# VectorE mends a row ahead of its share of the second list's sort, in the second half of each step

## What is computed

```python
a_src = (h * att_src).sum(-1)
a_dst = (h * att_dst).sum(-1)
e = leaky_relu(a_src[src] + a_dst[dst], negative_slope=0.2)
e_max = segment_max(e, dst)
ee = exp(e - e_max[dst])
denom = segment_sum(ee, dst)
alpha = ee / (denom[dst] + 1e-16)
agg = segment_sum(h[src] * alpha[:, :, None], dst) + b_gat
...
scores = layernorm(agg).mean(1)          # per expert
w = softmax(top_k(scores, 2))
out = sum over experts of g[e] * (gelu(x @ W1[e] + b1[e]) @ W2[e] + b2[e])
```

## Time and profile before

| what | us |
|---|---|
| median of 3 runs | 2843.73 |
| lowest and highest run | 2842.95, 2855.72 |
| profiled execution, its own time | 2834.66 |
| span of the profiled execution, first to last instruction | 2832.8 |
| busy: VectorE | 2124.0 |
| busy: GpSimd | 1202.6 |
| busy: TensorE matmul | 1002.3 |
| busy: ScalarE | 780.2 |

### The profile page before, as it was taken

The page is one execution under the profiler, slowest core; times in us unless marked ns, Lnnn a source line. Parts: engine busy times, 40 slices in busy tenths (PEclk is TensorE's granted clock), DMA queues, the critical chain, the costliest instruction groups (busy, mean ns, idle before and its releaser), DMA issues.

```text
span 2832.8 us, 22266 instructions
## 1 busy us (share of the span) xinstructions
PE 1002.3 (35%) x4867; PEld 675.7 (24%) x4867; DVE 2124.0 (75%) x4081; ACT 780.2 (28%) x1624; POOL 1202.6 (42%) x1234
## 2 busy tenths in 40 slices
PE   6778777499922110099543322350000000000000
PEld 3455445266611110066322221230000000000000
DVE  5989999999789992999488888875633412822888
ACT  3555555244411110044332222221000000000344
POOL 0000000000000005777777764777777777736750
PEclk8766777699955555599775666675555555555555
DMA  2222324992200002133231212124212113342676
GB/s 62 67 67 71 82 70 178 393 138 74 74 15 0 0 0 27 25 83 82 61 47 35 43 37 40 39 46 41 36 20 24 20 10 24 46 42 82 188 240 226
DMA packets 259502, 202.29 MB, mean 71 GB/s; under 512 B 101592, under 2 KB 207445, under 8 KB 258902
## 3 DMA queue, kind: packets, MB, share of 16 engines
q1 hardware_dynamic: 189766, 114.21, 17.2%
q0 software_dynamic: 46336, 44.61, 8.8%
q10 hardware_dynamic: 23314, 42.60, 4.7%
HBM read 94.51 MB, written 107.07 MB: 71 GB/s over the span
## 4 chain that ended last, share of the span: by engine, by line
DVE 28%; PE 21%; POOL 18%; DVEq 14%; issue 10%; ACT 5%; DMA 3%; ACTq 1%; SPq 0%; POOLq 0%
POOL sb_rows_g L782 16%; PE bank L1022 7%; DVE sb_xi L1678 7%; PE bank L1012 6%; DVEq L1694 5%; DVE sb_xi L1685 3%; DVE sb_inv L1383 2%; PE bank L938 2%; DVE sb_hid_y L1518 2%; DVEq L1414 2%; PE bank L1001 2%; DVEq L1404 2%; DVE sb_y_new L2172 1%; PE bank L1019 1%; DVE sb_new L1907 1%
## 5 line engine op out<-in xcount | busy, mean ns | idle before, releaser
L782 POOL DMA_INDIRECT sb_rows_g<-scr_node,sb_srcs x1024 | 1001.4, 978 | 312.1 <-issue 311.7
L1685 DVE TENSOR_TENSOR sb_xi<-sb_xi 128x512 f32<-128x512 f32 (+2 forms) x852 | 427.2, 568 | 46.7 <-ACT sb_xi L1171 33.0
L1001 PE MATMUL bank<-sb_ident,sb_xi 128*128 128x128 f32 x448 | 99.5, 410 | 532.6 <-DVE sb_xi L1685 280.3
L1678 DVE TENSOR_TENSOR sb_xi<-sb_xi 128x1024 f32<-128x1024 f32 (+2 forms) x258 | 243.5, 944 | 27.5 <-ACT sb_xi L1176 8.7
L1022 PE MATMUL bank<-sb_w,sb_hid_y 128*128 128x128 f32 x2048 | 262.6, 281 | 0.0
L782 POOL DMA_INDIRECT sb_hid_y<-scr_level,sb_row_at x8 | 7.9, 985 | 597.3 <-DVE sb_row_at L1442 595.1
L1012 PE MATMUL bank<-sb_tnT_in,sb_w 128*128 128x512 f32 x512 | 238.5, 618 | 57.7 <-DVE sb_sinks L1790 33.5
L1679 DVE TENSOR_TENSOR sb_xi<-sb_xi 128x1024 f32<-128x1024 f32 (+2 forms) x258 | 245.7, 952 | 0.0
L1022 PEld LDWEIGHTS bank<-sb_w,sb_hid_y 128*128 128x128 f32 x2048 | 238.2, 191 | 29.0 <-issue 29.0
L1194 ACT ACTIVATE sb_hid_y<-bank,sb_b1c 128x512 f32<-128x512 f32 x256 | 163.6, 691 | 233.4 <-PE bank L1012 231.5
L1001 PEld LDWEIGHTS bank<-sb_ident,sb_xi 128*128 128x128 f32 x448 | 85.6, 216 | 545.0 <-DVE sb_xi L1685 286.8
(11 more groups left out here) (340 smaller groups left out, 2127.0 us busy)
## 6 DMA issues: line engine op xcount, KB each, us to landing
scr_expert_out<-sb_y_new ACTq DMA_DIRECT2D x64, 512.0 KB, 3.8
sb_y_in<-scr_expert_out SPq DMA_DIRECT2D x32, 1024.0 KB, 6.7
scr_state<-sb_zeros POOLq DMA_DIRECT2D x6, 4096.0 KB, 55.5
sb_rows_g<-scr_node,sb_srcs POOLq DMA_INDIRECT x1024
scr_state<-sb_state SPq DMA_DIRECT2D x16, 768.0 KB, 6.4
scr_tnT<-sb_tnT SPq DMA_DIRECT2D x34, 256.0 KB, 2.0
sb_tnT_in<-scr_tnT ACTq DMA_DIRECT2D x34, 256.0 KB, 2.7
sb_xa<-in_x SPq DMA_DIRECT2D x64, 128.0 KB, 2.5
```

The lines of the kernel that those rows point to most:

```text
L782: pool.indirect_dma_start(to, None, table, bass.IndirectOffsetOnAxis(ap=index, axis=0), **kw).then_inc(s, 16)
L1001: last = pe.transpose(bank[b][:, m * P:(m + 1) * P], src[:, (4 * b + m) * P:(4 * b + m + 1) * P], ident[:, :])
L1678: dve.tensor_tensor(vb[:, :, 0], va[:, :, 0], va[:, :, 1], ALU.min)
L1685: last = dve.tensor_tensor(vb[:, :, d, :, c], va[:, :, d, :, 0], va[:, :, d, :, 1], ALU.min if c == d else ALU.max)
```

## The change

The two lines that mend in a second half now stand first in `half`, on both engines that take part: VectorE's `mend(k - 2)` ahead of the sort's levels and of the search's parts, and ScalarE's `fix_exponentials(k - 2)` ahead of the exchanges' copies and the experts' chunks. What an instruction does is unchanged, as is the number of instructions. The queues of GpSimd, SyncE and TensorE are in the same order as before. In the loop (steps 4 and 5) nothing stands between the old place and the new one, so those steps are unchanged. Four halves have another order: (2, 1) and (3, 1), where the mend passes two levels of the sort; (6, 1), where it passes `find_rank`; and (7, 1), where it passes `find_nodes` and `own_terms`.

```diff
             def half(k, u, j, pair, b):
+                if some(k) and u == 1 and (not isinstance(k, int) or k > 1):
+                    fix_exponentials(k - 2)
                 end = EXCHANGES + SORTED_BY.get((j, u), 0)
                 if end > done[0]:
                     exchanges(done[0], end)
...
-                if some(k):
-                    if u == 0:
-                        chain_exponentials(k - 1)
-                    elif not isinstance(k, int) or k > 1:
-                        fix_exponentials(k - 2)
+                if some(k) and u == 0:
+                    chain_exponentials(k - 1)
                 place_around(k, u, pair, 2 * b + u)
                 edge_exponentials(k, u)
...
             def half(k, u, j, pair, b):
+                if some(k) and u == 1 and (not isinstance(k, int) or k > 1):
+                    mend(k - 2, b)
                 end = SORTED_BY.get((j, u), 0)
                 if end > done[0]:
                     sort_levels(1, done[0], end)
...
-                if some(k):
-                    if u == 0:
-                        chain_runs(k - 1, 1 - b)
-                    elif not isinstance(k, int) or k > 1:
-                        mend(k - 2, b)
+                if some(k) and u == 0:
+                    chain_runs(k - 1, 1 - b)
                 edge_scans(k, u, j, pair, b)
```

## The result

The changed kernel takes **2804.59 us** (median of 4 runs, 2799.65 to 2811.89), the kernel before, on the same chip, 2843.34 us (median of 4 runs). The ratio is 0.9862, with a 95% interval of 0.9825 to 0.9899. The prediction said 2804.7 us, within 2794 to 2818. The profiled execution took 2799.65 us with a span of 2797.8 us, where that of before took 2834.66 us with 2832.8 us.

What follows compares the result with a forecast made beforehand. GpSimd's in-order gather queue was taken to bound the kernel, with one 40.6 us hole at a mended row's store. Filling it gains 37.6 to 40.6 us, taken as 39: median 2843.73 becomes 2804.7 us, range 2794 to 2818.

Steps and rivals of the forecast that it cites:

- What bounds: GpSimd's gather queue sets the pace; its one hole, 40.6 us at the first mended row's store, delays everything behind.
- The mend in (2, 1): On VectorE, begins at 1680.1 and fits the 1.95 us gap before the sort, delaying the sort 0.3 us.
- The store, the mend in (3, 1), and what is next: GpSimd's first store no longer waits; second mend ends 21.8 us ahead of its store; no new wait follows.
- The gathers that fill the hole: Beside the sort of (2, 1), 30 slightly slower gathers fill the hole; gain 37.6 to 40.6 us, taken as 39.
- The rule against the change: Skill's SBUF contention rule: if it held for gathers and sort, the hole takes hardly any gather, gain near 0.
- VectorE's cover: In half (5, 1) VectorE keeps 35 us of waiting as cover; each microsecond beyond is paid, slower than before from 74.
- the mend holds the sort: Rival, 2%: VectorE's early mend waits and delays the sort and later work; slower, for example 2860 us at 90 us lost.
- The sum of VectorE's waits for rows: Sign over the whole kernel: the sum stays more or less the same, (5, 0)'s wait gone, (5, 1)'s near 35 us.
- Halves (6, 1) and (7, 1): Mend passes parts of the search: 2 us earlier or less later, under row waits of 60.5 and 19.34 us.

Runs made afterwards that it cites:

- the second execution: The changed kernel run once more without any edit, in rounds with the kernel before: ratio 0.9877, stage (first search gather to last gather of rows) 1385.2 us.
- a hole of 11 us: Changed kernel with the mends of (2, 1) and (3, 1) between the sort's two levels: first store waits 11.13 us, ratio 0.9918 to the kernel before.
- the experiment with one move alone: Changed kernel with only the mend of (2, 1) moved, the others left late: ratio 0.9988 to the kernel before, second store waits 37.75 us.
- the ten gathers: Ten extra GpSimd gathers in half (1, 0), result unused: added to the kernel before, ratio 1.0010; added to the changed kernel, 0.9948 to the kernel before.
- 151 us: Changed kernel with 116 extra VectorE operations in half (5, 1), result unused, taking 150.9 us: ratio 1.0030 to the kernel before.
- 20 operations more: Changed kernel with 20 extra VectorE operations in half (5, 1), result unused: ratio 0.9871 to the kernel before.
- 60 more: Changed kernel with 60 extra VectorE operations in half (5, 1), result unused, 78.1 us in all: ratio 0.9888 to the kernel before.
- last mend earlier: Changed kernel with the mend of step 6 and its row's fetch also moved ahead of the trips behind the last rows: ratio 0.9846 to the kernel before.

## Why the prediction was right, and where it was not

*What bounds.* Right. Without the hole of 40.6 us the stage was 36.9 us shorter, and 30.0 us in the second execution. With one of the two moves the hole goes to the next store or stays, and a hole of 11 us costs 6 to 13.

*The mend in (2, 1).* Right: 1.9 us in VectorE's gap, with a delay of the sort of 0.2 us where 0.3 was taken. Its place, 1680.1, was off by 3.3 us, of which 2.5 are the later start of the stage.

*The store, the mend in (3, 1), and what is next.* Right: no store waits, the second mend ends 23 us ahead where 21.8 were forecast, and the experiment with one move alone shows 37.75 us of wait where the prediction worked out 1896.6 - 1859.1 = 37.5.

*The gathers that fill the hole.* Here the forecast had the terms wrong, though it did not show in the first time. It was 39 us, out of 37.6 to 40.6: of the 40.6 us the gathers beside the sort were to eat 1.6, at most 3.0. By the medians the first measurement gained 38.75 us; with the changed kernel again it was 31.6, and the stages of the two gained 36.9 and 30.0. Split at the first store, the stage shows where the rest went (us):

| | before | changed | changed, again |
|---|---|---|---|
| up to the first store, without its wait | 602.2 | 602.6 | 608.7 |
| from the first store on | 772.4 | 775.2 | 776.1 |

From the first store on, the changed kernel paid 2.9 and 3.7 us. But the 576 gathers of rows there took 0.2 us less and 0.5 us more than before: they cost nothing to speak of. What grew are transfers that had no term at all. The first gathers of a half (`sb_adw`) took 1.4 and 3.4 us more, and in the first execution the first two stores took 1.50 and 1.68 us instead of 1.02.

The second missing term is larger. Up to the first store the second execution took 6.5 us more than before, 6.3 of them in its gathers of rows, although both kernels have the same order of work there, but for the last 5 us or so, beside the moved mend. The prediction took GpSimd's arrival at the store from a single execution. Lateness ahead of the store is free in the kernel before, as the hole shrinks by it (the ten gathers show that), and is paid in the changed one. So the gain is the hole less what an execution happens to be late at the store: 30 to 37 us of stage is what the two executions show, and the 39 of the forecast lie above both.

*The rule against the change.* The gathers were not kept out: 28 went through in the former hole, at 1019 ns each. The price is the 8% over the quiet 946 ns, and 4% on one of the two kinds of the sort's long instructions. The prediction had set against the change what the Trainium skill says in "SBUF — State Buffer", section "Who interferes with whom", of VectorE instructions with two inputs in SBUF. The same section of the Trainium skill also says that in a probe `tensor_copy` was seen to stall DMA, but `tensor_tensor` was not. The sort's instructions are of the latter kind, and this trace agrees: a gather beside them took 73 ns more, while each of the long ones takes over 1200 ns.

*VectorE's cover.* This step failed, without harm to the forecast. In (5, 1) it was 45.4 us instead of 35, and 53.7 us in the second execution. In the first, six of the ten are the later rows (2.5 for the later start, 3.7 for the smaller gain); VectorE itself came 4 us earlier than worked out, though it started later, as its waits for SyncE's stores and flags in (3, 1) to (5, 0) had become 6 us shorter. More important, "beyond that each microsecond is paid" is wrong. It held one wait of VectorE for the end of the slack, though the next half has a wait of its own and GpSimd runs two halves ahead. What counts is the first thing that GpSimd needs from VectorE: 45.4 + 68.3 = 114 us could be hidden in the first execution, and the changed kernel is level with the one before only at about 114 + 37 = 151 us of lateness, not at 74. In the second execution 122 us could be hidden and 30 were gained, which makes 152. With 151 us it measured 1.0030, 1.0007 to 1.0054. The point from which the rival "the mend holds the sort" decides was thus twice as far away as the prediction had it. Both numbers are for lateness that begins in (5, 1); what a mend that held the sort in (2, 1) would meet on the way there wasn't tried.

*The sum of VectorE's waits for rows.* It was to stay more or less the same and fell from 210.0 to 180.8 us. That sign didn't fit the forecast's own numbers, by which (5, 0) and (5, 1) lose 41 us together. VectorE's work is the same and the stage 36.9 us shorter, so its idle time has to fall by about as much: 29 us at the rows and 6 at SyncE's stores and flags.

*Halves (6, 1) and (7, 1).* Right as far as it can be seen: moved alone they change nothing in the stage.

## What to carry to other kernels

On an engine whose queue is in order, a wait in the middle of the queue costs everything behind it: find what it waits for, ask whether that was ready long before, and move the producer, then follow the engine to its *next* wait, since one move alone only sends the stall on. To find how late a producer may come, don't stop at its own idle time: go to the first thing that the bounding engine needs from it, and add up the idle times on the way. And a stall that is removed takes its cover with it: what was late ahead of it was free before, and is paid now.

## What was not expected of the hardware

Kernels without the hole were less steady in the stage than those with it. With a hole of about 40 us in one of the two places it took 1412.9 to 1416.1 us; the changed kernel took 1378.2 and 1385.2, with 20 operations more 1377.8, with 60 more 1387.3. The difference is mainly in the gathers' own durations, and mainly ahead of the first store. Here is the group of the changed kernel's gathers over the whole span, first in the first profiled execution, then again:

```profile
L782 POOL DMA_INDIRECT sb_rows_g<-scr_node,sb_srcs x1024 | 1001.6, 978 | 312.1 <-issue 312.1
```

```profile
L782 POOL DMA_INDIRECT sb_rows_g<-scr_node,sb_srcs x1024 | 1008.2, 985 | 312.1 <-issue 312.1
```

The same instructions of the same kernel took 6.5 us more, and the stage was 7.0 us longer. In the eleven profiled executions without the ten extra gathers GpSimd worked 601.8 to 603.8 us up to the first store in eight, and 608.7 to 609.9 us in three. All three (changed again, 60 operations, last mend earlier) have no wait at the store, but the order of work up to VectorE's half (2, 1), some 5 us ahead of that point, is the same in all the kernels, so this may be chance. A hole at the first store hides such lateness. Why a gather takes longer in one execution than in another stays open. So does why the first store took 1.02 us at the end of the hole and anything between 1.01 and 1.51 us beside the sort.
